# A sparse-expert layer on one core: one more lap of four tiles written out ahead of the loop

## The reference

```python
logits = x @ router_weight.T + router_bias
top_val, top_idx = jax.lax.top_k(logits, TOP_K)          # 4 of 16 experts
router_scores = zeros.at[rows, top_idx].set(softmax(top_val))
gate_up = jnp.einsum('th,ehd->etd', x, gate_up_proj) + gate_up_proj_bias[:, None, :]
gate = jnp.minimum(gate_up[..., ::2], 7.0)
up = jnp.clip(gate_up[..., 1::2], -7.0, 7.0)
out = jnp.einsum('etd,edh->eth', (up + 1.0) * gate * sigmoid(1.702 * gate), down_proj) + down_proj_bias[:, None, :]
out = (out * router_scores.T[:, :, None]).sum(axis=0)
```

## Time and profile before

| what | us |
|---|---|
| median of 3 runs | 894.6 |
| lowest and highest of them | 886.27, 897.5 |
| the profiled execution | 891.88 |
| its span, first to last instruction | 890.0 |
| TensorE busy | 773.8 |
| VectorE busy | 595.0 |
| ScalarE busy | 403.4 |
| GpSimd busy | 318.3 |

### The profile page before, as it was taken

The page is one execution under the profiler, slowest core; times in us unless marked ns, Lnnn a source line. Parts: engine busy times, 40 slices in busy tenths (PEclk is TensorE's granted clock), DMA queues, the critical chain, the costliest instruction groups (busy, mean ns, idle before and its releaser), DMA issues.

```text
span 890.0 us, 16748 instructions
## 1 busy us (share of the span) xinstructions
PE 773.8 (87%) x3566; PEld 626.6 (70%) x3567; DVE 595.0 (67%) x1068; ACT 403.4 (45%) x663; POOL 318.3 (36%) x351
## 2 busy tenths in 40 slices
PE   4464737469899999999999999999999999999993
PEld 2134436357688888788888887878788878888882
DVE  4678789777567657677575857767766485775541
ACT  3998697532335225425253443543442254352221
POOL 1330657747232323334232332323432333232231
PEclk9765565559899999999999999999999999999997
DMA  8501121156553633674636647467547353723231
GB/s 277 208 0 48 48 49 49 48 175 181 142 133 89 182 69 97 171 214 111 172 102 173 175 97 223 109 174 214 171 108 211 71 159 91 210 66 69 49 61 29
DMA packets 70626, 111.80 MB, mean 126 GB/s; under 512 B 29878, under 2 KB 32182, under 8 KB 70518
## 3 DMA queue, kind: packets, MB, share of 16 engines
q1 hardware_dynamic: 32454, 74.22, 24.4%
q0 software_dynamic: 18336, 36.26, 20.7%
q10 hardware_dynamic: 19728, 0.15, 1.2%
HBM read 83.78 MB, written 28.90 MB: 127 GB/s over the span
## 4 chain that ended last, share of the span: by engine, by line
PE 65%; ACT 11%; DMA 9%; POOL 5%; issue 4%; SPq 2%; DVE 1%; ACTq 1%; DVEq 0%; POOLq 0%
PE gate_up_ps L854 36%; PE bank L854 21%; DMA xg<-xn_rows,gslot 4%; PE bank L836 3%; ACT bgu L520 3%; ACT marks L520 3%; PE bank L844 3%; POOL slot_rows L393 2%; POOL out_dram L437 2%; ACT x_sb L533 1%; DMA bd_raw<-_ffn_down_proj_bias_dram 1%; PE gate_up_ps L743 1%; DMA out_dram<-x_sb 1%; DMA bgu<-n_gate_up_proj_bias_dram 1%; ACT A L530 1%
## 5 line engine op out<-in xcount | busy, mean ns | idle before, releaser
L854 PE MATMUL gate_up_ps<-w,xh 128*128 (+1 forms) x1152 | 365.5, 399 | 0.3 <-DVE xl L1034 0.3
L437 POOL DMA_INDIRECT out_dram<-yb,aslot x72 | 132.6, 1842 | 425.8 <-ACT yb L638 397.1
L854 PEld LDWEIGHTS gate_up_ps<-w,xh 128*128 128x128 f32 x1152 | 213.1, 190 | 41.5 <-issue 0.5
L854 PE MATMUL gate_up_ps<-w,xl 128*128 (+1 forms) x576 | 227.0, 394 | 0.0
L854 PE MATMUL bank<-w,hh 128*128 (+1 forms) x576 | 180.3, 394 | 7.3 <-DVE hl L1039 6.3
L631 ACT ACTIVATE sg<-gc 128x512 f32<-128x512 f32 x72 | 45.6, 634 | 222.5 <-DVE gc L1049 222.5
L1045 DVE TENSOR_TENSOR gu<-gate_up_ps,bgu 128x1024 f32<-128x1024 f32 x72 | 88.2, 1224 | 72.6 <-PE gate_up_ps L854 72.2
L854 PEld LDWEIGHTS bank<-w,hh 128*128 128x128 f32 x576 | 107.8, 189 | 35.3 <-issue 13.4
L1039 DVE TENSOR_TENSOR hl<-bank,hh 128x512 fp32r<-128x512 f32 x72 | 49.6, 688 | 117.1 <-ACT hh L625 117.1
L854 PEld LDWEIGHTS gate_up_ps<-w,xl 128*128 128x128 f32 x576 | 109.2, 190 | 23.7
L625 ACT CAST hh<-bank 128x512 fp32r<-128x512 f32 x72 | 42.3, 587 | 159.9 <-PE bank L844 158.9
(11 more groups left out here) (209 smaller groups left out, 797.6 us busy)
## 6 DMA issues: line engine op xcount, KB each, us to landing
raw_w<-_L_ffn_gate_up_proj_dram SPq DMA_DIRECT2D x64, 512.0 KB, 4.3
raw_w<-in_L_ffn_down_proj_dram SPq DMA_DIRECT2D x64, 256.0 KB, 5.7
bgu<-n_gate_up_proj_bias_dram SPq DMA_DIRECT2D x16, 512.0 KB, 7.1
x_sb<-in_x_dram SPq DMA_DIRECT2D x4, 1024.0 KB, 11.5
xn_rows<-xn SPq DMA_DIRECT2D x4, 1024.0 KB, 5.6
out_dram<-x_sb SPq DMA_DIRECT2D x4, 1024.0 KB, 6.3
xg<-xn_rows,gslot POOLq DMA_INDIRECT x74, 5.4
out_dram<-yb,aslot POOLq DMA_INDIRECT x72, 4.8
```

Of the source, the lines that this page charges most:

```text
L437: pool.indirect_dma_start(out_v, bass.IndirectOffsetOnAxis(aslot[:, k, 0:1], 0), yb[:, k % 2, :], None, bounds_check=TOKENS - 1, oob_is_er ...
L854: last = nc.tensor.matmul(out_ps, lhs[:, rows], w[:, bass.ds(buf, 1), part, c, cols].rearrange("p a d -> p (a d)"), start=(m == 0), stop=( ...
```

## The change

The first lap of the loop, lap 15 with tiles 60 to 63, is written out as the ones before it, on PE, DVE, ACT and POOL alike; the loops begin at lap 16, tile 64. So that the loop always has a lap to run, the last tile's number is held at 64 or more, in the second operation of the instruction that makes `total_i`; the bound of `final` that the program is told is one higher too. Should there be fewer than 65 tiles, the surplus ones would be empty. `FROZEN` stays 4, and `SURE` stays 15, since the edit adds 1 where it is used.

```diff
@@ final_lap
-            return eng.value_load(laps_tab[0:1, 0:1], min_val=SURE, max_val=LAPS - 1)
+            return eng.value_load(laps_tab[0:1, 0:1], min_val=SURE + 1, max_val=LAPS - 1)
@@ pool, and the same on act, pe and dve
-            for T in range(FROZEN, UNROLL * SURE):
+            for T in range(FROZEN, UNROLL * (SURE + 1)):
                 step(T, T % UNROLL)
-            with pool.Fori(SURE, final + 1) as lap:
+            with pool.Fori(SURE + 1, final + 1) as lap:
                 for k in range(UNROLL):
                     step(UNROLL * lap + k, k)
@@ vector, the tile table
-            send(V.tensor_scalar(total_i[:], cum[:, E - 1:E], -1.0, None, ALU.add))
+            send(V.tensor_scalar(total_i[:], cum[:, E - 1:E], -1.0, float(UNROLL * (SURE + 1)), ALU.add, ALU.max))
```

More of the change, by code:

```diff
@@ L693, in _ @@
             final = final_lap(act)
-            for T in range(FROZEN, UNROLL * SURE):
+            for T in range(FROZEN, UNROLL * (SURE + 1)):
                 step(T, T % UNROLL)
-            with act.Fori(SURE, final + 1) as lap:
+            with act.Fori(SURE + 1, final + 1) as lap:
                 for k in range(UNROLL):
@@ L901, in _ @@
             final = final_lap(pe)
-            for T in range(FROZEN, UNROLL * SURE):
+            for T in range(FROZEN, UNROLL * (SURE + 1)):
                 step(T, T % UNROLL)
-            with pe.Fori(SURE, final + 1) as lap:
+            with pe.Fori(SURE + 1, final + 1) as lap:
                 for k in range(UNROLL):
@@ L1276, in _ @@
             final = final_lap(dve)
-            for T in range(FROZEN, UNROLL * SURE):
+            for T in range(FROZEN, UNROLL * (SURE + 1)):
                 step(T, T % UNROLL)
-            with dve.Fori(SURE, final + 1) as lap:
+            with dve.Fori(SURE + 1, final + 1) as lap:
                 for k in range(UNROLL):
```

## The result

| | median us | lowest to highest | runs |
|---|---|---|---|
| before | 891.57 | 885.36 to 897.5 | 20 |
| changed | 897.31 | 889.82 to 900.23 | 20 |

The changed kernel is slower by 0.6%: ratio 1.006, 95% interval 1.0042 to 1.0079, that is 3.7 to 7.0 us. I forecast 0.2 us of gain. Within the 2% bound it is "no change"; but single runs scatter by over 10 us, and twenty of each tell 0.6% from nothing.

A forecast was written before the change was run, and what follows sets the result against it. The prediction took TensorE's stream of matmuls to bound the kernel. Its terms, -0.19 us and otherwise 0, took the profiled 891.88 us to 891.7, given as 894.4 us against the median of 894.6; range 886 to 899.

The forecast's parts named there:

- Part 1: Tiles 60 to 63 written out: the issue wait ahead of TensorE's `down` in step 60 falls from 0.21 to 0.02, -0.19 us.
- Part 2: Loop entered at tile 64 instead of 60: setting TensorE's counter takes 33 ns, hidden by its sequencer's lead; 0 us.
- Step 64 keeps its 0.20: Step 64, still in the loop, keeps 0.20 us of issue ahead of TensorE's `down`.
- Part 3: One jump back fewer on TensorE, VectorE, ScalarE and GpSimd: 0 us; without cover, 0.25 us at most.
- Parts 4 and 5: VectorE's clamp of `total_i` beneath tile 0's matmuls, 0 us, at most 0.15; DMA issues and SyncE's stream unchanged, 0 us.
- Rival B: Loop jumps cost more than their rows, engines waiting for code; removing one gains at most 0.53 us, giving 894.1; chance 0.07.
- Rival C: Written-out code supplied late to TensorE's sequencer in steps 60 to 63: +5.8 us, giving 900.4; chance 0.06.

The follow-up runs named there:

- lap 11: Kernel before with the loops of all four engines begun at lap 11 (tile 44), seven laps in the loop; ratio to before 1.0014.
- padding of 100: Changed kernel with 100 idle semaphore increments at the start of ScalarE's stream; ratio to before 1.0007.
- padding of 256: Changed kernel with 256 idle semaphore increments at the start of ScalarE's stream; ratio to before 1.0182.
- of 68: Kernel before with 68 idle semaphore increments at the start of ScalarE's stream; ratio to before 1.0089.
- of 84: Kernel before with all loops begun at lap 11, plus 84 idle semaphore increments at the start of ScalarE's stream; ratio to before 1.0185.

## Why the prediction was wrong

- *Part 1, -0.19 us in step 60:* right to the hundredth, 9.57 to 9.38, by the step that was named, "issue" 0.21 to 0.03.
- *Part 2, the loop entered at tile 64, 0 us:* TensorE's own entry cost nothing. But I had the entry on TensorE in view and not what the written-out code of tile 63 would be on VectorE: +0.30 us, by a stop of 0.42 us between two register rows. "Step 64 keeps its 0.20" was wrong by that.
- *Part 3, one jump back fewer, 0 us:* this step failed. I priced the jump by the rows of TensorE and wrote for the others "I take no more than that". ScalarE's jump was not read, and above all a jump's price was taken as a property of the instruction. It is a property of where its loop lies: 0.25 us at the old place and 2.4 us at the new one, +4.03 us on TensorE's path with the clock. Which wait would end late next (`hl` behind `hh` behind ScalarE's register rows) could have been named from the trace of before: at its jump into lap 17 ScalarE's register rows and loads ran from 835.8 to 838.0 us, and `hh` came at 838.12, 1.1 us after the transposes that it waits for had begun, where most steps have 0.6 to 0.8. So ScalarE has no lead there, unlike TensorE's own sequencer, which runs 2.1 us ahead.
- *Parts 4 and 5:* nothing seen of either; `total_i` took 146 ns.
- *Rival B* had the right mechanism with the wrong sign, and cited the rule that decides. I dismissed it since the trace of before showed no reload. But that trace shows a loop that happened to fit; the change moves the loop by 324 instructions on ScalarE, so it was no evidence for the place after. By that rule there are two cases, not one, and the second is a loss: a loop that fitted and no longer does.
- *Rival C* had the sign right and the place wrong: it looked for code supplied late in the written-out lap, on TensorE.
- *The range* held the 897.31 us (886 to 899), and "within 2%" was right. That is luck: the range came from the scatter of three runs, and nothing in it stood for this cost. The sign was not forecast, and a slowdown by this mechanism had no chance of its own. An estimate from the blocks of the Trainium skill's page, "Runtime: NRT & Kernel Launch", section "Instruction fetch mechanics": 345 instructions fit into two blocks of 256 from 168 of 256 starts, and of the 168 places at which the loop of before could lie, 68 don't fit once moved on by 324. That is a chance of 0.4, which I gave to nothing.

## What to carry to other kernels

When an edit changes the length of the code ahead of a loop, count the loop's body on each engine and ask whether it is still all at hand at the jump back; the stretch's instruction-queue packets tell it in one look, and a trace in which a jump is free says nothing of the same jump elsewhere. Idle instructions where the engine waits anyway can put a loop back on a good place: here 100 on ScalarE took the ratio from 1.006 to 1.0007, which can't be told from 1. Price a jump on the engine that has no lead, not on the one that has most to do.

## What the runs showed of the hardware

- A jump back on ScalarE costs 0.20 to 0.25 us from the branch to the next row when its loop is at hand, and 2.4 to 2.7 us when not. Starts without a stall were 3533, 4829 and 5253 by the built program's order; starts with one 3617, 4897, 5153 and 5409, the last two 256 apart. At each of the eleven stalled jumps a packet of q14 starts 0.9 to 1.2 us after the branch.
- The code of ScalarE comes in pieces, and their edges can be seen. In the changed kernel its stream stops for 0.32 to 0.33 us between two sequencer rows at 458.8, 475.2, 565.5, 732.9, 789.9 and 806.7 us, with a packet of q14 of 8 KB some 0.7 us after five of the six stops (0.8 after the other). The program's order isn't quite the stream on the chip: in the trace a DMA issue is two rows and an unconditional jump of ScalarE none. Recounted so, a lap is 316 instructions and the loop 344, and the six stops lie whole multiples of 128 instructions apart. Counted from such an edge, the loop begins at 13, 29 and 45 in the kernels without a stall (before, lap 11, padding of 100), and at 73, 73, 81 and 113 in those with one (changed, padding of 256, of 68, of 84).
- The Trainium skill's rule on taken branches (page "Runtime: NRT & Kernel Launch", section "Instruction fetch mechanics") agrees with this, and so do its two blocks of 256, if their edges are at every second of these steps of 128. But what is loaded at a time holds 128 here, half such a block, and the runs don't tell two blocks of 256 from four pieces of 128.
- TensorE's, VectorE's and GpSimd's loops never showed such a stall at their jumps back, in any run.
- After nearly the same idle time (2.0 to 2.15 us) TensorE's granted clock sometimes fell to its lower level and sometimes didn't, with 1.6 to 1.7 us between the two.
- An idle semaphore increment at the start of ScalarE's stream takes some 80 ns (20.4 us for 256, against the start of the changed kernel).
